# Multi-query attention: score products on 32-row tiles of TensorE, the mask added in VectorE's maximum, biases as one rounded product

## What is computed

```python
x = x + layernorm(attn(layernorm(x)))      # the stage that this case is about
x = x + layernorm(layers(layernorm(x)))    # six layers of windowed attention and gated FFN
# attn: 16 heads of 8 features; one K and one V of 8 features for all heads
Q = (x @ Wq + bq).reshape(B, S, 16, 8); K = x @ Wk + bk; V = x @ Wv + bv
A = where(causal, einsum('bhqd,bkd->bhqk', Q, K), -inf)
P = softmax(A / sqrt(8)); O = einsum('bhqk,bkd->bhqd', P, V)
return O.reshape(B, S, 128) @ Wo + bo
```

## Time and profile before

| | us |
|---|---|
| median of 3 runs (lowest to highest) | 3566.55 (3564.18 to 3569.26) |
| the profiled execution's own time | 3564.89 |
| its span in the trace | 3563.1 |
| busy: PE / PEld / DVE / ACT / POOL | 3346.0 / 2794.2 / 2975.9 / 2700.0 / 2602.3 |
| mean granted clock of TensorE, of full speed | 0.983 |

### The profile page before, as it was taken

One profiled execution on the slowest core, in us unless ns is written; L12 is line 12 of the kernel. 1 busy time (PEld: TensorE's weight loads), 2 busy tenths in 40 slices (PEclk: granted clock), 3 DMA queues, 4 the chain that ended last, 5 costly groups with the idle time before them and its releaser, 6 DMA issues. The chain is left out here.

```text
span 3563.1 us, 158627 instructions
## 1 busy us (share of the span) xinstructions
PE 3346.0 (94%) x66450; PEld 2794.2 (78%) x66450; DVE 2975.9 (84%) x4073; ACT 2700.0 (76%) x4132; POOL 2602.3 (73%) x3291
## 2 busy tenths in 40 slices
PE   7999848999999999999999999999999999999995
PEld 5666537888888888788888788887888888888884
DVE  6777548888888888988888888889888889888884
ACT  4666527888887888888888788887888887888873
POOL 4566567777777777777777777777777777777773
PEclk9999959999999999999999999999999999999997
DMA  2000012322223222223222232222232222222222
GB/s 59 4 7 7 7 33 75 89 65 68 66 69 95 71 71 66 63 67 94 71 71 71 66 94 66 65 70 71 76 86 69 70 65 71 71 69 65 66 67 65
DMA packets 161740, 228.22 MB, mean 64 GB/s; under 512 B 42258, under 2 KB 60632, under 8 KB 161496
## 3 DMA queue, kind: packets, MB, share of 16 engines
q1 hardware_dynamic: 161624, 226.85, 23.8%
HBM read 21.00 MB, written 4.19 MB: 7 GB/s over the span
## 5 line engine op out<-in xcount | busy, mean ns | idle before, releaser
L1124 POOL TENSOR_TENSOR by_cos<-by_cos,by_sin 128x1024 f32<-128x1024 f32 x384 | 911.3, 2384 | 14.3 <-DVE by_sin L1478 14.3
L1130 POOL TENSOR_TENSOR by_cos<-by_cos,norms 128x1024 f32<-128x1024 f32 x384 | 734.3, 1912 | 13.0
L1476 DVE TENSOR_TENSOR by_cos<-proj,turns 128x1024 f32<-128x1024 f32 x384 | 470.2, 1225 | 182.5 <-ACT squares L1366 152.7
L1210 PE MATMUL proj<-qkv_hi,xs_hib 128*128 128x512 f32 x1152 | 512.1, 445 | 48.6 <-DVE by_sin L1478 39.5
L1478 DVE TENSOR_TENSOR by_sin<-proj,turns 128x1024 f32<-128x1024 f32 x384 | 466.3, 1214 | 0.0
L1482 DVE TENSOR_REDUCE sumsb<-squares 128x16 f32<-128x1024 f32 x384 | 464.5, 1210 | 1.5 <-DVE w_lo L1545 1.5
L1366 ACT ACTIVATE squares<-proj 128x1024 f32<-128x1024 f32 x384 | 393.3, 1024 | 86.6 <-PE proj L1212 86.3
L1212 PE MATMUL proj<-qkv_hi,xs_lob 128*128 128x512 f32 x1152 | 458.1, 398 | 0.0
L1211 PE MATMUL proj<-qkv_lo,xs_hib 128*128 128x512 f32 x1152 | 457.7, 397 | 0.0
L1219 PE MATMUL ring<-ident,by_cos 128*128 128x128 f32 x3072 | 386.1, 274 | 8.9 <-DVE xT L1579 5.5
L1346 ACT ACTIVATE vb<-proj 128x1024 f32<-128x1024 f32 x192 | 195.2, 1017 | 254.6 <-DMA v_win<-vb 200.7
(11 more groups left out here) (186 smaller groups left out, 8020.8 us busy)
## 6 DMA issues: line engine op xcount, KB each, us to landing
v_win<-vb SPq DMA_DIRECT2D x1152, 128.0 KB, 2.3
v_win<-vb SPq DMA_DIRECT2D x768, 64.0 KB, 2.0
in_qkv<-L_ffn_Wqkv SPq DMA_DIRECT2D x12, 768.0 KB
wo<-L_ffn_Wo SPq DMA_DIRECT2D x6, 512.0 KB, 4.3
x_tok<-L_attn_x SPq DMA_DIRECT2D x8, 256.0 KB, 4.1
residual<-x_tok SPq DMA_DIRECT2D x8, 256.0 KB, 2.0
o_x<-residual SPq DMA_DIRECT2D x1, 2048.0 KB, 7.8
out<-o_x SPq DMA_DIRECT2D x8, 256.0 KB, 2.2
```

What stands on the lines that cost most here:

```text
L1124: nc.gpsimd.tensor_tensor(both, both, by_sin[:, j, :], ALU.add).then_inc(e[f"{w_}_added"].sem, 1)
L1130: nc.gpsimd.tensor_tensor(heads, heads, inverse, ALU.mult).then_inc(e[f"{w_}_ready"].sem, 1)
L1210: nc.tensor.matmul(out, xs_hi[:, tile], qkv_hi[:, cols], start=True, stop=False)
L1476: nc.vector.tensor_tensor(of_heads(by_cos[:, t % 2, j, :]), heads, table(0), ALU.mult)
```

## The change

Keys are no longer copied: a head's products use the 32 rows of its slot in queries and keys (a 32x128 tile of the array), and ACT writes the transposed keys straight into `kT`. The mask leaves PE: DVE adds it (now f32) in the operation that finds the maximum, one for each query tile, so that every head has three fills. The negated maxima move from DVE to POOL, with the keys' slots 24 and 25 as 1 and -1. The biases are split into high and low parts once, into rows 0 and 1 of a tile of 128 rows, and enter by one fp32r product. In the last steps (n >= 122) normalising and adding the outputs move from POOL to DVE.

```diff
-PAIR_FILLS = 5
+FILLS = 3
+NO_SCORES = HEADS - AHEAD
@@ fills
-    first = PAIR_FILLS * (m // 2)
-    return ((3, first), (2, first + 1), (1, first + 2)) if m % 2 == 0 else ((3, first + 3), (2, first + 4))
+    return (3, FILLS * m), (2, FILLS * m + 1), (1, FILLS * m + 2)
@@ sync: biases go to two rows, that of the output with them
+                sp.dma_start(bias_in[:, at:at + n], weights[b_].rearrange("(a n) -> a n", a=1).broadcast_to([2, n]))\
+                    .then_inc(w_loaded, 16)
...
@@ gpsimd
-            def spread_keys(b, i):
...
+            def negated_maxima(group):
+                b, g = group // GROUPS, group % GROUPS
+                heads = slice(g * PER_GROUP, (g + 1) * PER_GROUP)
+                pool.wait_ge(s_max, PER_GROUP * FILLS * (group + 1))
+                pool.wait_ge(q_full, group + 1)
+                nc.gpsimd.tensor_scalar(qa[b % 2][:, :, heads, 24], row_max[:, :, heads], -1.0, None,
+                                        ALU.mult).then_inc(m_hi, 1)
+                pool.wait_ge(m_hi, group + 1)
+                nc.gpsimd.tensor_tensor(qa[b % 2][:, :, heads, 25], row_max[:, :, heads],
+                                        qa[b % 2][:, :, heads, 24].bitcast(F32), ALU.add).then_inc(m_done, 1)
...
                 if 0 <= n < HEADS:
                     causal(n)
+                if h % PER_GROUP == 1 and 0 <= (n + AHEAD) // PER_GROUP < B * GROUPS:
+                    negated_maxima((n + AHEAD) // PER_GROUP)
...
-                        normal_output(old, (0, 1))
-                    elif h == 15:
-                        normal_output(old, (2, 3))
+                    if h in (14, 15) and n < NO_SCORES:
+                        normal_output(old, (0, 1) if h == 14 else (2, 3))
@@ tensor, scores
+                rows = slice(SLOTS * i, SLOTS * i + SLOTS)
-                queries = lambda k: qT0[:, g, k * P:(k + 1) * P]
+                queries = lambda k: qT0[rows, g, k * P:(k + 1) * P]
...
+                    last = nc.tensor.matmul(out[:, :], queries(3), keys[rows, :], start=True, stop=True)
...
+                    last = nc.tensor.matmul(out[:, 0:2 * P], queries(1), keys[rows, 0:2 * P], start=True, stop=True)
-                nc.tensor.matmul(masked, ident_bf[:, :], mask, start=False, stop=True,
-                                 skip_group_check=True).then_inc(s_full, 1)
+                last.then_inc(s_full, 1)
@@ tensor, scoresT
-                    last = nc.tensor.matmul(scoreT[k][:, at:at + width], kT[b % 2][:, i, kt * P:(kt + 1) * P],
-                                            qT1[:, g, kt * P:S], start=True, stop=True)
+                    last = nc.tensor.matmul(scoreT[k][:, at:at + width], kT[b % 2][rows, kt * P:(kt + 1) * P],
+                                            qT1[rows, g, kt * P:S], start=True, stop=True)
@@ tensor, project (project_out likewise)
-                nc.tensor.matmul(out, ones[0:1, 0:P], bqkv[0:1, :].unsqueeze(1).broadcast_to([1, 2, QKV_W]),
+                nc.tensor.matmul(out, ones_r[:, :], bias[:, 0:QKV_W].unsqueeze(1).broadcast_to([P, 2, QKV_W]),
@@ scalar, keys_turned
-                at_least(act, keys_done, PER_GROUP * b)
-                copy(k_flat[:, :], near[:, :]).then_inc(k_flat_done, 1)
+                at_least(act, st_full, 3 * MQA_H * (b - 1))
+                copy(kT[b % 2][:, :], near[:, :]).then_inc(keys_done, 1)
@@ vector
+            def split_biases():
+                dve.wait_ge(w_loaded, 16 * 7)
+                nc.vector.tensor_copy(bias_hi[:, :], bias_in[:, :]).then_inc(bias_done, 1)
...
+                nc.vector.scalar_tensor_tensor(out=bias[0:2, :], in0=bias_hi[:, :].bitcast(F32), scalar=minus_row[:, 0:1],
+                                               in1=bias_in[:, :], op0=ALU.mult, op1=ALU.add).then_inc(bias_done, 1)
+            def normal_output(b):
...
+            def add_output(b):
...
+            def normal_sum(b):
...
@@ vector, maxima
+                at_least(dve, s_max, fill - FILLS + 1)
+                def largest(qt, at):
+                    n = (qt + 1) * P
+                    place = slice((fill % FILLS) * S + at, (fill % FILLS) * S + at + n)
+                    return nc.vector.tensor_tensor_reduce(
+                        out=masked[:, place], in0=score[fill % 2][:, at:at + n], in1=mask_qk[:, 4 * P - n:4 * P], scale=1.0,
+                        scalar=LOWEST, op0=ALU.add, op1=ALU.max, accum_out=row_max[:, qt, h:h + 1])
+
+                last = largest(qt, 0)
+                if qt == 2:
+                    last = largest(0, 3 * P)
                 last.then_inc(s_max, 1)
-            def negated_maxima(group):
...
```

More of the change, by code:

```diff
@@ L164, in mqa_stage @@
         no_max = sem("no_max")
[L165 removed]
+        k_full, keys_done = sem("k_full"), sem("keys")
         q_full, q_done = sem("q_full"), sem("q")
@@ L383, in scores @@
-                nc.tensor.matmul(masked, ident_bf[:, :], mask, start=False, stop=True,
-                                 skip_group_check=True).then_inc(s_full, 1)
+                    nc.tensor.matmul(out[:, 0:3 * P], queries(2), keys[rows, 0:3 * P], start=True, stop=True)
+                    last = nc.tensor.matmul(out[:, 3 * P:4 * P], queries(0), keys[rows, 0:P], start=True, stop=True)
+                else:
+                    last = nc.tensor.matmul(out[:, 0:2 * P], queries(1), keys[rows, 0:2 * P], start=True, stop=True)
@@ L668, in sum_statistics, with normal_tile @@
                 statistics(2, b, tiles_of(b), t)
+            def normal_tile(norm, b, out, in_, t):
+                return nc.vector.tensor_scalar(out, in_, stat[:, norm, b, t, 0:1], rstd[:, norm, b, t:t + 1],
+                                               ALU.subtract, ALU.mult)
+            def normal_output(b):
+                dve.wait_ge(rstd_done[1], b + 1)
+                for t in range(TILES):
+                    last = normal_tile(1, b, o[:, t, :], o[:, t, :], t)
+                last.then_inc(o_done, 1)
+            def add_output(b):
+                dve.wait_ge(o_done, b + 1)
+                four = x_tok[:, b * TILES:(b + 1) * TILES, :]
+                nc.vector.tensor_tensor(four, four, o[:, :, :], ALU.add).then_inc(x2_done, 1)
+            def normal_sum(b):
+                dve.wait_ge(rstd_done[2], b + 1)
+                dve.wait_ge(yT_full, b)
+                for t in range(TILES):
+                    last = normal_tile(2, b, y[:, t, :], x_tok[:, b * TILES + t, :], t)
+                last.then_inc(y_done, 1)
             def lo_parts(b, u):
@@ L743, in _ @@
                         variance(1, old)
+                    elif h == 15 and n >= NO_SCORES:
+                        normal_output(old)
                 if batch_of(older):
-                    if h in (1, 2, 3):
+                    if h == 0 and n >= NO_SCORES:
+                        add_output(older)
+                    elif h in (1, 2, 3):
                         sum_statistics(older, h - 1)
@@ L750, in _ @@
                         variance(2, older)
+                    elif h == 11 and n >= NO_SCORES:
+                        normal_sum(older)
 QKV = 3 * INNER
```

112 lines of the change are left out of this document (37 added, 75 removed).

## The result

The changed kernel takes 3651.3 us (median of 4 runs, 3643.5 to 3652.1); before took 3565.4 us in the runs beside it. The ratio is 1.0236, with a 95% interval of 1.0223 to 1.0249: slower by 86 us, where 3530 was forecast. The profiled execution took 3651.57 us, its span 3649.6.

A forecast was written before the change was run, and what follows sets the result against it. PE was taken to bound a batch, DVE and POOL close behind. Batches -28.5, ends -6.2 and start -1.8 sum to -36.5 us; from 3564.9 that gives 3528.4, forecast as 3530 us, range 3503 to 3555.

The forecast's parts named there:

- C: Rival, DVE in every step: maxima with a second walk take over the batch, +50 us, 3617 us; chance 0.12.
- B: Rival, score products on PE: row tiles don't overlap, 1.37 us a step, 3544 us or 3553; chance 0.19.
- A: Rival, heads: overlap and maxima at their good ends, 0.75 us on PE, 1.63 on DVE, 3507 us; chance 0.20.
- D: Rival, POOL's chain and waits for negated maxima: 2 to 3 us a batch lost, 3555 to 3562 us; chance 0.07.
- Score products: PE in the heads: 1.1 us a step by overlapping row tiles, -0.34 us in odd and -0.9 in even steps.
- Biases: Projection and output biases on PE in one rounded pass: 0.53 us twice and 0.82 once, 1.9 us a batch.
- Ends: After the last heads: normalising and adding on DVE, a shorter mask wait and the bias, -6.2 us.
- Start: Start of the kernel: two bias products at half clock shrink, -1.8 us.
- Maxima on DVE: Heads: four maxima a head with the mask added in the same operation, 2.0 us a head.
- Switches of tile shape: PE in the heads: 0.18 us a switch, bounds 0 and 0.3; one or two more in steps with other PE work.
- The layers: Six layers and output stage after the attention: unchanged at 3103 us.

The follow-up runs named there:

- e1: Changed kernel with score products back on 128 rows and keys copied four times by POOL, rest of the change kept; 3562.08 us, ratio 0.9988.
- e6: e8 with the third plain score product of a step issued behind the step's other TensorE work; 3540.10 us, ratio 0.9923.
- e8: e1 with the negated maxima back on DVE instead of POOL; 3555.67 us, ratio 0.9964.
- e10: e1 with each score product on 64 rows of the array instead of 128; 3603.36 us, ratio 1.0110.
- e7: Kernel before with only the rounded one-pass biases, and the last normalisations and additions on DVE instead of POOL; 3548.66 us, ratio 0.9947.
- e5: Changed kernel with a step's transposed products on the same 32 rows as its plain ones, so none overlap; 3687.43 us, ratio 1.0329.
- e3: Changed kernel with three redundant 512-column bf16 products a head on 32 rows, ahead of the third plain product; 3605.2 us, one execution.
- e4: Changed kernel with each step's transposed products issued first, then the plain ones, meant to prevent overlap; 3709.9 us, one execution.
- e2: Changed kernel with three redundant 512-column bf16 products a head on 128 rows, ahead of the third plain product; 3590.9 us, one execution.

## Why the prediction was wrong

**The step that failed.** It is the first: "There the TensorE (PE) clock is 1.00 while the heads run". That number was read as a property of the stage and was one of its matmuls. Every duration of the stage was taken at 2.4 GHz, no bound or rival had the clock in it, and the products were then put on a quarter of the rows. At 0.75 the stage takes 471.6 us; with full-height tiles and all else of the change kept, 381.7. These 89.9 us, what the clock takes less what the overlap gives, are the bulk of the miss. Against the span that was forecast (3563.1 - 36.5 = 3526.6) the profiled one is 123.0 longer: 89.9 for the narrow tiles in the heads, 21.1 by which e1's 381.7 us exceed the forecast 360.6, 2.5 at the start, 2.4 behind the heads, 7.1 in the layers. Of the 21.1, the wait for the first maximum is the part that was found: e6, which hides it, has 358.3 us, under the forecast of 360.6, and without any overlap. A hint stood in the rows: the clock is 0.96 and 0.69 in the last two stretches of the earlier trace rows. The only half clock that the prediction reckons with is that of the bias products at the start. The layers' small tiles, in a stage whose clock is 0.99, spoke against a danger.

**The rivals.** The chance of slower was 0.12, all of it for C, and C is refuted: a maximum of 512 columns takes 688 ns, the accumulator's read is listed with 83 ns, and the next operation starts 0.62 us after it (338.88 to 339.50 us in DVE's timeline). Four maxima a head come to 1.65 us from start to start, not 2.0 and far from 2.5. B is refuted by the timeline, where two products start at once; its price for eight products in sequence, 1.37 us, was right (1.39 in e6). A had its ends right for the pieces, seven of the eight products under way in 0.57 us and the maxima at 1.65, and the step wrong even at full clock: 1.42 us, not 0.75 and not the forecast's 1.1. D had the place, and far too high a price: POOL's chain holds h3 in e1 by 1.1 us a batch, against 0.7 in before, and e8 gets 0.5 of it back.

**The terms, at full clock.**
- *Score products:* -0.34 us in odd and -0.9 in even steps. Measured in a step with nothing else, at full clock: 1.42 us, that is -0.02 against the odd step's 1.44 and -0.6 against the even step's 2.0. On 64 rows e10 gains nothing over e1 with the clock set aside. In the prediction "DVE's 2.0 to 2.5 us just fits below them"; it did not ask what waits for the first of these maxima. TensorE does, in front of every third fill, 7.0 us a batch in e1 and e8. In the step at 338.32 us the way is 0.56 us from the step's start to the maximum, 0.62 for it and 0.13 to the third product, 1.31 before TensorE can go on, and that, not TensorE's columns, sets the length of the step.
- *Biases:* -1.9 us a batch; e7's batch is 2.30 us shorter (50.45 to 48.15) with hardly anything else changed in it. Right, a little low. (The even steps of the sum come to -3.5 and not -3.6, which changes nothing.)
- *Ends:* -6.2; 43.2 to 36.4 us in e7, -6.8. Right. In the changed kernel -3.8, at a clock of 0.52.
- *Start:* -1.8; 41.4 to 39.5 us in e7, -1.9. Right.
- *Maxima on DVE:* too dear by 0.35 us a head, with little effect on the time: it is the first maximum that TensorE waits for, and that one was priced at about 0.7 us and takes 0.62.
- *Switches of tile shape:* 0.18 us. In e10 the first weighted value starts 0.31 us after the product on fewer rows before it (252.90 and 253.21 us), as it did after a full-height one. A change of rows adds nothing there that can be seen. Between transposes and narrow products it costs what was priced: the four transposes of the values occupy 0.53 us up to the next narrow product in the changed kernel (337.79 to 338.32) and 0.35 up to the next full-height one in before (285.75 to 286.10), +0.18.
- *The layers:* "stay as they are". They do not. They took 3089.4 us before and 3096.5 after, and 3098.3 to 3100.8 in e1, e6 and e7. Each is one execution, and those of one kernel differ by some us (before: 3563.2 to 3569.3), so the 7.1 by itself is not clear of that, nor are the 4.4 of e5 and the 5.5 of e10; the 9 to 11 us of e1, e6 and e7 are harder to put down to it.

The last point was followed in the traces. With the same instruction of ScalarE found in both, e6 is 3.7 us ahead of before at 2896 us into the layers (3369.60 us in before's timeline, 3327.03 in e6's) and 9.5 behind at their end. In the stretch between, the same 128 small products on 64*32 tiles take one piece before and are cut in e6 (TensorE's timeline, before and e6):

```profile
3473.40 1.56 PE L1238 MATMUL score<-kTb,qTb 64*32 64x64 f32 x128 [0.31 <-ACT score L1346]
```

```profile
3434.96 1.27 PE L1279 MATMUL score<-kTb,qTb 64*32 64x64 f32 x97 [0.31 <-ACT score L1387]
3438.82 0.68 PE L1279 MATMUL score<-kTb,qTb 64*32 64x64 f32 x31 [2.58 <-issue]
```

The clock of the last 135 us of the span is 0.85 before and 0.82 in e6 and in e1, but in e7 it is 0.85 as well, and e7's layers lose 8.9 us all the same: the clock is not shown to be the cause. What the 2.58 us of "issue" are was not found, and why the versions that reach the layers earlier than before (e1, e6, e7) lose 9 to 11 us there stays open.

**Open besides.** Why three narrow bf16 products a head (e3) lift the clock from 0.75 to 0.87, when the narrow f32 products do not hold it even back to back (e5): their type, passes or place were not varied. So the runs show that narrow products take the clock down, and not by what measure of TensorE's work.

## What to carry to other kernels

A granted clock of 1.00 in the profile belongs to the work that ran under it. Before matmuls are moved to fewer rows of the array, price the stage at half clock as a rival of its own, and after the change read the clock first: untouched products slow down with the changed ones. And when TensorE gets faster, ask which product waits for a result of its own step; issuing that one last gave 2.5 us a batch here, where the overlap of 64-row tiles gave nothing until then.

## What the runs showed of the hardware that was not expected

- The granted clock of the heads against the rows that the score products take: 0.75 on 32 rows, 0.70 on 32 rows without overlap, 0.95 on 64 (in the shortest of five executions), 0.99 on 128; with a full-height filler beside the 32-row products 0.99. The 128 rows of e1 are zero in the keys outside the head's own 32, so it is the rows that a tile takes up that count here, and not those that add to the result.
- Matmuls on other rows start ahead of their place in the program. In e4 the plain product of 512 columns started 0.01 us after the transposed one, though three transposed products stood between them. The Trainium skill (TensorE: Matmul & The Clock Gate, Part 2, Step-by-step: what each phase is for) says that only weight loads are pulled forward and that matmuls stay in program order; the trace does not agree. On the same rows (e5) they start in order. That an engine does its instructions in the order written, as the part on the kernel before has it, is thus not true of these matmuls.
- An addition with a running maximum on VectorE is as fast as the plain reduction, 688 ns for 512 columns against 0.68 us, and the read of its accumulator, 83 ns by its own row, costs nothing from start to start.
- Weight loads on 32-row tiles take as long as those on 128 rows. Loads ahead of the transposed products in the heads, before (clock 1.00, mean 197 ns) and in e2 (32 rows, clock 0.99, mean 189 ns); the changed kernel has 227 ns at its clock of 0.75:

```profile
L395 PEld LDWEIGHTS a_scoreT<-a_qT,a_kT 128*128 128x128 f32 x509 | 89.1, 197 | 4.4 <-issue 2.2 <-ACT a_probs L528 2.0
```

```profile
L395 PEld LDWEIGHTS a_scoreT<-a_qT,a_kT 32*128 32x128 f32 x508 | 85.6, 189 | 24.6 <-issue 15.0 <-ACT a_probs L528 1.7
```
